# Partial sums of a state-space scan: 224 additions on GpSimd become accumulating DMAs, under a new order of all engines

## What is computed

```python
def step(h, ins):                       # 256 steps, per sequence; h is [256 channels, 16 states]
    d_t, B_t, C_t, u_t = ins
    dA = jnp.exp(d_t[:, :, None] * A)
    h = h * dA + (d_t * u_t)[:, :, None] * B_t[:, None, :]
    y = jnp.einsum('bds,bs->bd', h, C_t)      # sum over the 16 states of h * C
    return (h, y)
...
y = ys.transpose(1, 0, 2) + xm * D_ssm
y = y * jax.nn.silu(res)
return y @ out_w.T + out_b
...
x = x + 0.5 * ffn(layernorm(x))
x = x + attn(layernorm(x))              # Mamba block, Mamba block, memory
x = x + 0.5 * ffn(layernorm(x))
```

## Time and profile before

| | |
|---|---|
| median of three runs | 1960.4 us |
| profiled execution, its own time | 1957.8 us |
| its span from first to last instruction | 1955.9 us |
| TensorE busy | 1511.4 us |
| VectorE busy | 1723.2 us |
| ScalarE busy | 1142.5 us |
| GpSimd busy | 755.6 us |
| mean granted TensorE clock | 0.865 of full speed |
| DMA over the span | 14.45 MB, mean 7 GB/s |

### The profile page before, as it was taken

How to read it: one execution, slowest core, us unless ns; L and a number is a source line. 1 busy time by engine, 2 the same in 40 slices (tenths; PEclk the granted TensorE clock), 3 DMA queues, 4 the chain that set the end, 5 groups by cost and what they waited for, 6 DMA issues and landing times. The chain is left out here.

```text
span 1955.9 us, 26508 instructions
## 1 busy us (share of the span) xinstructions
PE 1511.4 (77%) x8672; PEld 1313.5 (67%) x8672; DVE 1723.2 (88%) x2421; ACT 1142.5 (58%) x2206; POOL 755.6 (39%) x366
## 2 busy tenths in 40 slices
PE   5778547878878787878888787887888888548778
PEld 4667435777767676767677667776777777437667
DVE  4269999999989998999989999899989999999941
ACT  3276555566756665656666566665755657436522
POOL 0005354444434354454325354353434454443310
PEclk9889767879989889998989898988889799668879
DMA  5000000000000000000000000000000000000000
GB/s 182 1 6 1 1 1 1 6 1 1 1 13 1 1 1 7 6 1 1 1 8 6 1 1 7 7 1 1 1 6 1 1 1 1 6 1 1 1 6 6
DMA packets 11688, 14.45 MB, mean 7 GB/s; under 512 B 400, under 2 KB 8592, under 8 KB 11408
## 3 DMA queue, kind: packets, MB, share of 16 engines
q1 hardware_dynamic: 11536, 12.56, 2.0%
HBM read 10.46 MB, written 2.10 MB: 6 GB/s over the span
## 5 line engine op out<-in xcount | busy, mean ns | idle before, releaser
L1101 POOL TENSOR_TENSOR acc<-acc,G 128x1024 f32<-128x1024 f32 x192 | 557.9, 2905 | 467.6 <-DVE G L922 461.4
L912 DVE TENSOR_TENSOR_SCAN hs<-dA,dbu 128x1024 f32<-128x1024 f32 x256 | 646.4, 2543 | 3.1 <-issue 2.2
L566 ACT ACTIVATE raw<-b_h 128x512 f32<-128x512 f32 x512 | 305.0, 598 | 340.7 <-PE b_h L328 324.8
L623 ACT ACTIVATE dA<-delta,A 128x255 f32<-128x255 f32 x1024 | 422.7, 495 | 55.3 <-DVE hs L912 35.8
L405 PE MATMUL b_r<-bcr,selr 128*128 128x256 f32 x1024 | 245.5, 343 | 199.8 <-DVE G L922 118.5
L405 PEld LDWEIGHTS b_r<-bcr,selr 128*128 128x128 f32 x1024 | 184.0, 217 | 249.3 <-DVE G L922 134.5
L922 DVE TENSOR_TENSOR G<-hs,b_r 128x1024 f32<-128x1024 f32 x256 | 309.9, 1211 | 9.6 <-issue 3.0
L902 DVE TENSOR_TENSOR dbu<-du,b_r 128x1024 f32<-128x1024 f32 x256 | 308.2, 1209 | 0.4
L326 PE MATMUL b_h<-xh,w1h 128*128 128x512 f32 x512 | 242.4, 473 | 83.7 <-DVE xa L838 27.9
L335 PE MATMUL b_h<-w2s,raw 128*128 128x128 f32 x2048 | 279.7, 292 | 0.0
L335 PEld LDWEIGHTS b_h<-w2s,raw 128*128 128x128 f32 x2048 | 269.3, 209 | 1.1
(11 more groups left out here) (144 smaller groups left out, 1652.8 us busy)
## 6 DMA issues: line engine op xcount, KB each, us to landing
xin<-x_dram SPq DMA_DIRECT2D x8, 256.0 KB, 2.9
raw<-w_dram SPq DMA_DIRECT2D x1, 2048.0 KB, 11.2
out_dram<-ob SPq DMA_DIRECT2D x8, 256.0 KB, 2.3
prm<-pack_dram SPq DMA_DIRECT2D x1, 1124.5 KB, 5.2
hs<-sel_dram SPq DMA_DIRECT2D x2, 512.0 KB, 12.4
G<-sel_dram SPq DMA_DIRECT2D x2, 512.0 KB, 7.6
dA<-early_dram SPq DMA_DIRECT2D x1, 512.0 KB, 11.5
dbu<-early_dram SPq DMA_DIRECT2D x1, 384.0 KB, 11.7
```

The costliest lines, as they stand in the source:

```text
L566: do(hT[e % 2][:, c, :], H[i % 2][:, :], ACT.Silu).then_inc(f_hact, 1)
L623: last = do(dA[j % 4][:, d, k, 1:], delta[b][:, k, 1:], ACT.Exp, scale=A[:, k, s:s + 1])
L912: V.tensor_tensor_scan(flat(hs[j % 2]), flat(dA[j % 4]), flat(dbu[j % 2]), 0.0, ALU.mult, ALU.add)\
L1101: Q.tensor_tensor(acc[b][:, :, :, :], (G[0] if j == 1 else acc[b])[:, :, :, :], G[j % NG][:, :, :, :], ALU.add).then_inc(q_gs, 1)
```

## The change

The additions on GpSimd go: `pair_sum` now issues a DMA on GpSimd's queue that adds `G[j % 3]` onto `acc[b]` in SBUF. Product 0 is written by VectorE straight into `acc[b]`, so there are still seven additions a pass. Each DMA waits for the one before to have landed. A landed DMA counts 16 on `q_gs`, so the waits of VectorE on it are multiplied by 16. GpSimd's hardware loop over groups 1 to 5 is written out. And the table `ORDER` is new for all engines; of it only four lines are shown.

```diff
     "vector": (
-        "gate flow b0 flog ftop b1 s0 s1 g0 b2 g1 b3 s2 s3 fweights g2 b4 low f0 s4 f1 g3 b5 g4 s5 b6 g5 b7 "
-        "delta mask s6 g6 s7 g7 xb f2",
+        "b0 b1 flow s0 gate flog ftop g0 s1 b2 g1 fweights s2 b3 g2 low s3 b4 f0 g3 s4 f1 b5 g4 delta s5 mask b6 "
+        "g5 s6 b7 g6 s7 xb g7",
...
     "gpsimd": (
...
-        "rms a1 a2 rs lnx rmsx a3 a4 a5 a6 a7",
+        "rms a1 rs lnx a2 a3 rmsx a4 a5 a6 a7",
...
             def scan_output(g, i, j):
...
-                last = j - NG if j >= NG else max(p for p in range(NP) if p % NG == j) - NP
-                wait(dve, q_gs, q * (NP - 1) + (max(last, 1) if last >= 0 else last + 1))
-                V.tensor_tensor(G[j % NG][:, :, :, :], hs[j % 2][:, :, :, :], spread_rows(i, (1, j)), ALU.mult)\
+                if j:
+                    last = j - NG if j > NG else max(p for p in range(1, NP) if p % NG == j % NG) - (NP - 1)
+                    wait(dve, q_gs, (q * (NP - 1) + last) * 16)
+                to = G[j % NG] if j else acc[i % 2]
+                V.tensor_tensor(to[:, :, :, :], hs[j % 2][:, :, :, :], spread_rows(i, (1, j)), ALU.mult)\
                     .then_inc(q_G, 1)
 
             def gate_y(g, i):
                 q, b = 4 * g + i, i % 2
-                dve.wait_ge(q_gs, (q + 1) * (NP - 1))
+                dve.wait_ge(q_gs, (q + 1) * (NP - 1) * 16)
...
                 pool.wait_ge(q_G, q * NP + j + 1)
-                if j == 1:
-                    wait(pool, q_yg, q - 1)
-                else:
-                    pool.wait_ge(q_gs, q * (NP - 1) + j - 1)
-                Q.tensor_tensor(acc[b][:, :, :, :], (G[0] if j == 1 else acc[b])[:, :, :, :],
-                                G[j % NG][:, :, :, :], ALU.add).then_inc(q_gs, 1)
+                wait(pool, q_gs, (q * (NP - 1) + j - 1) * 16)
+                Q.dma_start(acc[b][:, :, :, :].rearrange("p d h t -> p (d h t)"),
+                            G[j % NG][:, :, :, :].rearrange("p d h t -> p (d h t)"),
+                            accum_op=ALU.add).then_inc(q_gs, 16)
...
-            with pool.Fori(1, GROUPS - 2) as g:
+            for g in range(1, GROUPS - 2):
                 run(g, g * 2, g * 2 + 1, g * 2 + 2, False)
```

More of the change, by code:

```diff
@@ L46 @@
     "tensor": (
[8 rows of a table removed]
-    "scalar": (
[4 rows of a table removed]
-    "vector": (
[8 rows of a table removed]
[8 rows of a table added]
+    ),
+    "scalar": (
[4 rows of a table added]
+    ),
+    "vector": (
[8 rows of a table added]
+    ),
     "gpsimd": (
         "a1 a2 a3 a4 a5 a6 a7",
[3 rows of a table removed]
[3 rows of a table added]
+    ),
 }
```

## The result

The changed kernel takes 1803.4 us (median of 4 runs, 1800.3 to 1805.3) against 1960.5 for the kernel before: a ratio of 0.9196, 95% interval 0.9181 to 0.9212. A later set of runs of the same kernel gave 1807.9 (0.9218, 0.9197 to 0.9238). The profiled execution took 1800.3 us with a span of 1798.5.

What follows compares the result with a forecast made beforehand. VectorE was taken to bound the kernel before and after; -128 + 5 + 21 - 19 + 20 + 4 = -97 us on the profiled 1957.8, with the median 2.6 higher, gave 1863 us, range 1815 to 2000.

Steps and rivals of the forecast that it cites:

- stretching gone: VectorE's scans, `du`, `delta` and `xn` no longer lengthened by GpSimd's adds: 132 us, less 4 for small instructions, -128 us.
- logits covered: In slot 0 the gate and a scan now cover VectorE's wait for the experts' logits: about 7 x 2.7, -19 us.
- gates and the end: Gates wait for the last landing where slot 3 meets slot 0, +5 us; the last gate of the program, +4 us.
- VectorE waits more, TensorE above all: With TensorE at 44.8 of 52 us a slot, VectorE waits for it more: +20 us, chosen between 0 and +90.
- slots without expert work: 4 of 32 slots, 46.1 us in the mean, do not shrink and the shorter grow, limited by landings: +21 us.
- low end of 1818: All 132 us gained, logits covered, no new TensorE wait, 5 + 4 for gate and end, short slots unchanged: 1818 us.
- L: Length of an accumulating DMA, from a product's end to the next one's release: 5.5 us, between 3.6 and 7.6.
- cycle of a slot: Seven chained landings plus the way from gate to g1: 47.4 us at 5.5 a landing, under VectorE's 52.1.
- B (TensorE): Rival: TensorE takes over as the bound, `b_r` waits for products, +90 instead of +20: 1933 us; chance 0.12.
- C: Rival: GpSimd's own work on issuing 224 DMAs still holds VectorE up, 58 us: 1921 us; chance 0.10.
- A: Rival: the DMA landings become the bound, gates wait several us in every slot, 2058 to 2192 us; chance 0.19.

Runs made afterwards that it cites:

- e6: The changed kernel with two GpSimd powers of 128x4 ahead of each accumulating DMA: 2260.6 us.
- e9: The changed kernel with two small GpSimd adds of 128x4 ahead of each accumulating DMA: 1963.4 us.
- e5: The changed kernel with one GpSimd power of 128x4 ahead of each accumulating DMA: 2006.8 us.
- e13: The changed kernel with one small GpSimd add of 128x4 ahead of each accumulating DMA: 1884.9 us.
- e4: The kernel before with the new order and each GpSimd add cut to 4 of 1024 columns, sums over the states left out: 1790.2 us.
- e3: The kernel before, old order kept, with each GpSimd add cut to 4 of 1024 columns, sums over the states left out: 1835.3 us.

## Why the prediction was wrong

**The bound and the mechanism were right.** VectorE set the pace before and after, and the adds' hidden price was the larger part of what the change removed. By term, in the profiled executions:

| term | predicted, us | found, us |
|---|---|---|
| stretching gone | -128 | -137.9 (VectorE busy) |
| logits covered | -19 | -28.1 (40.5 to 12.4) |
| gates and the end | +5 and +4 | +5.3 (3.6 to 8.9) |
| VectorE waits more, TensorE above all | +20 | +3.3 (all other idle time) |
| slots without expert work | +21 | none: they shrank |
| sum | -97 | -157.4 |

**The steps that failed.** The largest two are charges of the sum that did not come, +21 and +20: 41 of the 60 us between 1803.4 and the predicted 1863. "They don't shrink, and the shorter grow": in group 7 the two slots went from 44.5 and 47.7 to 41.8 and 44.1. The gates' starts:

```profile
1481.65 0.69 DVE L930 TENSOR_TENSOR yg<-acc 128x512 f32<-128x512 f32 x1
...
1523.40 0.69 DVE L930 TENSOR_TENSOR yg<-acc 128x512 f32<-128x512 f32 x1 [1.13 <-DMA acc<-G]
...
1567.55 0.69 DVE L930 TENSOR_TENSOR yg<-acc 128x512 f32<-128x512 f32 x1 [0.75 <-DMA acc<-G]
```

I had charged them the mean way from gate to g1, 8.9 us, with the routing steps in it that these slots don't have, and a step of 5.5. They wait 1.1 and 0.8 us for landings, no more. Since the gate's place in the table differs from slot to slot, I took the four slots from first `dbu` to first `dbu` as well: together 199.9 us before and 184.0 after, the full 4.0 us a slot. The other charge, +20 for new waits on TensorE, had nothing behind it but that TensorE would be busier; it is (85% of the steady stretch, 1066 of 1250 us), and VectorE doesn't wait for it more than before.

The other terms were short, and these took the time below the range as well. I had cut the stretching from 132 to 128 for GpSimd's small instructions, which were guilty of next to nothing; the four kinds of instruction lost 131 of the 137.9, and 4 more came from `un`, `ln` and the other `xn`, which I had left out. The logits gave 28.1 instead of 19. The place was right: slot 2's waits stayed at 0.9 us each. But I had taken the mean of both slots, 2.7, for slot 0, where from group 1 on they were 3.8 to 5.2 and are now at most 0.5. The low end of 1818, rounded to 1815, already had neither charge in it; against it the stretching gave 5.9 more, the logits 9.1, and gate and end cost 3.7 less, with 3.3 of other idle time against them. That is the 15 us down to 1803.

**The step of the chain, L,** was put at 5.5. It is 5.1 in the median (4.5 to land, 0.5 to the next issue) and 5.4 in the mean, so the size was right, though its parts were guesses. The model around it held far from the edge and failed near it. I took the cycle of a slot to be 7 L plus 8.9 us and the slot to be the larger of this and VectorE's 52.1. With the mean step of e6, 7.87, the cycle gives 2253 us for the kernel (1960.4 and 32 slots' cycle less 1755, as in the prediction); measured are 2261. With those of e9 and e5 it gives 1922 and 1962; measured are 1963 and 2007. In e13, at 6.01, it gives no loss at all; measured are 81 us more than the change. There VectorE's own pace is 50.8 us a slot (the change's, from gate to gate in groups 1 to 5), the cycle 7 x 6.01 and a measured 8.2, which is 50.3, and the slot takes 53.3. Averages over unlike slots hid this: in those groups the gates of the passes of slots 0, 2 and 3 wait mostly 2 to 6 us each, those of slot 1 not at all. Also, products 1 to 5 of a pass come some 6 us apart, slower than the landings, and the chain can't make use of that time.

What the prediction owes to luck is that the step stayed on the near side of this edge: with 0.6 us more in the mean (e13) it would have cost 81 us, and nothing in its model said so. No run has a mean step between 5.44 and 6.01, so where the loss begins is open.

**The rivals.** B (TensorE) and C (GpSimd's issuing holds VectorE up) did not happen: the rows of 0.69 us above exclude C, though GpSimd issues for 196 us. A didn't decide at the measured step. The old order with the same DMAs (e1), at the same step of 5.1, shows what A described: gates that wait in all 32 slots.

Open is why the new order gains as much as 45 us when additions are free (e4 against e3): some two thirds of it are spread over waits of a few us each, which no run here takes apart.

## What to carry to other kernels

When an engine's durations spread far above their minimum while nobody waits, look for the other engine that reads the same memory at those moments; moving its work to DMAs freed the first here without touching it. Work given to DMAs in a dependent chain trades bandwidth for latency: count the landings in the cycle, take the mean of the step and not its median, look at each slot and not at their average, and move the reader of the result back by a landing, or the gain is lost (here 1803 against 1997 us). Change and order have to be judged together: each alone lost 1.8 to 1.9%.

## What the runs showed of the hardware

- An accumulating DMA of 512 KB within SBUF, issued by GpSimd, occupies GpSimd 0.86 us, lands 4.5 us after issue, and the next dependent one goes out 0.5 us later. A plain copy lands after 2.9. The Trainium skill's fit for such DMAs ("DMA: Bandwidth & Descriptors", Anatomy of one DMA), 3.2 us, is near the copy; the DMA engines' share of the span, 34.4% against 16.1%, is what a second stream to be read would give, though no run here parts the reading from the adding.
- An instruction of GpSimd behind such a DMA, with a drain before it, stood until the DMA had landed. GpSimd in the changed kernel:

```profile
883.33 0.86 POOL L1098 DMA_DIRECT2D acc<-G  x1 [4.18 <-DMA acc<-G]
883.89 0.74 POOL L1066 TENSOR_TENSOR rstd<-mv,epst 128x4 f32<-128x4 f32 x1
888.26 1.04 POOL L1068 TENSOR_TENSOR rstd<-rstd,powh 128x4 f32<-128x4 f32 x1 [3.62 <-DMA acc<-G]
889.27 0.90 POOL L1098 DMA_DIRECT2D acc<-G  x1
```

The first half of the root runs at once, the second, behind the drain, 3.6 us later, on the landing. In the whole run this holds for 20 roots: each second half that stood behind a DMA still under way began 0.2 to 0.4 us after its landing. 13 of them lost 39.8 us so; VectorE waited 8.0 us for these roots (`xn`), against 3.2 before.
